# Two load queues at the start, three pairs' normalisation moved to the fourth step, one statistics block moved up in the tail

## What is computed

```
x = x + Wo(softmax(q k^T / 8) v),  q = layernorm(x) Wq,  k = ctx Wk,  v = ctx Wv
logits = layernorm(x) phi_w^T + phi_b            # (8, 56, 64, 32)
D = softmax over slots, C = softmax over experts
Xt = tanh(layernorm(clip(sum over tokens of D * layernorm(x))))
x = x + sum over slots of C * (Xt expert_w + expert_b)
```

## Time and profile before

| | |
|---|---|
| median of 3 runs | 428.83 us (427.79 to 429.29) |
| the profiled execution's own time | 429.79 us |
| its span (first to last instruction) | 428.0 us |
| mean granted clock | 0.996 |
| busy: PE, DVE, ACT, POOL | 98%, 78%, 58%, 39% |

### The profile page before, as it was taken

The page is one execution under the profiler, slowest core; times in us unless marked ns, Lnnn a source line. Parts: engine busy times, 40 slices in busy tenths (PEclk is TensorE's granted clock), DMA queues, the critical chain, the costliest instruction groups (busy, mean ns, idle before and its releaser), DMA issues.

```text
span 428.0 us, 7292 instructions
## 1 busy us (share of the span) xinstructions
PE 417.5 (98%) x2912; PEld 380.0 (89%) x2912; DVE 333.5 (78%) x613; ACT 247.1 (58%) x413; POOL 168.8 (39%) x99
## 2 busy tenths in 40 slices
PE   6999999999999999999999999999999999999987
PEld 4898999999999999889999998889999888999966
DVE  3788847877886768777898779978897899678891
ACT  2577546675566466646664666646755565556652
POOL 4509800516450405031706134536344634436810
PEclk8999999999999999999999999999999999999999
DMA  6401021114021001210110002000110000098000
GB/s 191 141 32 15 20 72 14 36 49 116 14 25 62 20 12 15 73 18 14 14 73 19 14 8 78 21 12 5 11 20 0 14 12 7 26 247 233 2 2 21
DMA packets 15417, 19.03 MB, mean 44 GB/s; under 512 B 4032, under 2 KB 10960, under 8 KB 15384
## 3 DMA queue, kind: packets, MB, share of 16 engines
q1 hardware_dynamic: 15384, 18.57, 17.4%
HBM read 18.31 MB, written 0.26 MB: 43 GB/s over the span
## 4 chain that ended last, share of the span: by engine, by line
PE 73%; DVE 16%; ACT 7%; DMA 1%; POOL 1%; issue 1%; SPq 0%; POOLq 0%; DVEq 0%
PE turned L745 14%; PE acc L765 8%; PE acc L767 7%; PE acc L766 7%; PE scores L729 7%; PE scores L735 7%; PE scores L732 7%; DVE small L1442 5%; DVE pT_l L1452 4%; ACT prob L1192 4%; PE misc L782 3%; PE misc L651 2%; ACT pT_h L1185 1%; PE misc L810 1%; DMA ctx_raw<-in_ctx_dram 1%; PE scores L1105 1%
## 5 line engine op out<-in xcount | busy, mean ns | idle before, releaser
L1185 ACT CAST pT_h<-turned 125x512 fp32r<-125x512 f32 x168 | 95.2, 590 | 123.4 <-PE turned L745 122.7
L1452 DVE TENSOR_TENSOR pT_l<-turned,pT_h 125x512 fp32r<-125x512 f32 x168 | 112.4, 686 | 56.6 <-ACT pT_h L1185 55.6
L1442 DVE TENSOR_REDUCE small<-scores 128x1 f32<-128x500 f32 x168 | 107.7, 673 | 3.7 <-PE scores L735 3.3
L745 PE MATMUL turned<-ident,prob 128*125 128x128 f32 x672 | 94.4, 276 | 2.0 <-DVE pT_l L1452 1.7
L745 PEld LDWEIGHTS turned<-ident,prob 128*125 128x125 f32 x672 | 87.5, 187 | 9.7 <-DVE pT_l L1452 3.9
L765 PE MATMUL acc<-pT_h,ctx_nh 125*128 125x256 f32 (+1 forms) x288 | 94.9, 330 | 0.0
L1192 ACT ACTIVATE prob<-scores,small 128x1500 f32<-128x1500 f32 x56 | 84.9, 1517 | 11.2 <-DVE small L1445 11.0
L767 PE MATMUL acc<-pT_h,ctx_nl 125*128 125x256 f32 (+1 forms) x288 | 86.5, 300 | 0.0
L766 PE MATMUL acc<-pT_l,ctx_nh 125*128 125x256 f32 (+1 forms) x288 | 86.3, 300 | 0.0
L729 PE MATMUL scores<-ctx_th,qk_h 128*128 128x500 f32 x168 | 70.3, 418 | 0.4 <-ACT prob L1192 0.4
L735 PE MATMUL scores<-ctx_th,qk_l 128*128 128x500 f32 x168 | 65.3, 389 | 0.0
(11 more groups left out here) (222 smaller groups left out, 552.6 us busy)
## 6 DMA issues: line engine op xcount, KB each, us to landing
ctx_raw<-in_ctx_dram SPq DMA_DIRECT2D x7, 750.0 KB
rbc<-rden_row SPq DMA_DIRECT2D x15, 128.0 KB, 3.5
rbc<-rden_row SPq DMA_DIRECT2D x8, 192.0 KB, 3.0
eb<-in_L_ffn_expert_b_dram SPq DMA_DIRECT2D x4, 256.0 KB, 5.9
ctx_raw<-in_ctx_dram SPq DMA_DIRECT2D x3, 224.0 KB, 6.0
wq_sb<-in_L_xattn_Wq_dram SPq DMA_DIRECT2D x2, 256.0 KB, 4.8
wk_sb<-in_L_xattn_Wk_dram SPq DMA_DIRECT2D x2, 256.0 KB, 5.9
wv_sb<-in_L_xattn_Wv_dram SPq DMA_DIRECT2D x1, 512.0 KB, 3.5
```

Of the source, the lines that this page charges most:

```text
L745: last = tr(turned[0:CK, m, 128 * c:128 * c + 128], prob[u][:, CK * j:CK * j + CK], ident[:, :])
L1185: nc.scalar.copy(pT_h[0:CK, PLACES[g // NT % 2][t], CPB * k:CPB * k + CPB, :], turned[0:CK, (KB * u + k) % 2, :].rearrange("p (c r) -> p c ...
L1442: m = v.tensor_reduce(bankmax[:, u, k:k + 1], scores[:, k, 0:KW], AX.X, ALU.max)
L1452: v.tensor_tensor(pT_l[0:CK, place, dst, :], turned[0:CK, (KB * u + k) % 2, :].rearrange("p (c r) -> p c r", c=CPB), pT_h[0:CK, place, dst ...
```

## The change

- Loads: SP loads x's first pair alone, Wq's first half, ctx rows 0 to 111 of all chunks in one transfer, the second halves of Wq and Wk, x's other pairs, Wv, Wo. ScalarE's queue issues Wk's first half and ctx rows 112 to 124. A turn of the first ctx waits for both parts of ctx, where it waited for its own chunks and the rest. SP's wait before Wv goes.
- The first weight turned is Wk (ScalarE copies it), then Wq (VectorE). The head pairs come before the first ctx turn; the first x turn goes to bank M0. The fillers are 6 of 128 columns in place of 3 of 256, and one more follows the x turn. VectorE's low query part comes before the second ctx part.
- The other pairs: VectorE's statistics move from the beginning to the step t = 3 of b = 0; POOL adds eps, takes the root and applies them between `split_weights` and `split_ctx(1, 1)`, where it did so before `split_ctx(0, 0)`.
- The tail: `slot_stats(3)` follows `slot_stats(2)`, before the wait for the expert bias and `add_expert_bias(0)`.

```diff
@@ SP
-            sp.dma_start(x_sb[:, :, :], x_v).then_inc(x_in, 16)
+            sp.dma_start(x_sb[:, 0:1, :], x_v[:, 0:1, :]).then_inc(x_in, 16)
             sp.dma_start(wq_sb[:, 0:HW], Wq[:, 0:HW]).then_inc(wq_in[0], 16)
-            sp.dma_start(wk_sb[:, 0:HW], Wk[:, 0:HW]).then_inc(wk_in[0], 16)
-            sp.dma_start(ctx_raw[ROWS0:CK, :, :], ctx_v[0][ROWS0:CK, :, :]).then_inc(ctx0_rest_in, 16)
-            for k in range(KB):
-                chunks = slice(CPB * k, CPB * k + CPB)
-                sp.dma_start(ctx_raw[0:ROWS0, chunks, :], ctx_v[0][0:ROWS0, chunks, :]).then_inc(ctx0_in[k], 16)
+            sp.dma_start(ctx_raw[0:ROWS0, :, :], ctx_v[0][0:ROWS0, :, :]).then_inc(ctx0_in[0], 16)
             sp.dma_start(wq_sb[:, HW:INNER], Wq[:, HW:INNER]).then_inc(wq_in[1], 16)
             sp.dma_start(wk_sb[:, HW:INNER], Wk[:, HW:INNER]).then_inc(wk_in[1], 16)
-            sp.wait_ge(ctx0_in[KB - 1], 16)
+            sp.dma_start(x_sb[:, 1:NQ, :], x_v[:, 1:NQ, :]).then_inc(x_rest_in, 16)
@@ POOL
             root(0, 0, 1)
-            root(1, 1, NQ)
-            pool.wait_ge(ln_rs, 2)
+            split_ctx(0, 0, first=True)
+            split_qk(1)
+            split_weights()
+            pool.wait_ge(rest_mv, 1)
+            gp.tensor_scalar(lnvar[:, 1:NQ], lnmv[:, 1:NQ, 1], EPS, None, ALU.add).then_inc(rest_var, 1)
+            pool.wait_ge(rest_var, 1)
+            gp.tensor_tensor(lnrs[:, 1:NQ], lnvar[:, 1:NQ], neghalf[0:PT, 1:NQ], ALU.pow).then_inc(rest_rs, 1)
+            pool.wait_ge(rest_rs, 1)
             for q in range(1, NQ):
                 last = gp.tensor_scalar(xn[:, q, :], x_sb[:, q, :], lnmv[:, q, 0:1], lnrs[:, q:q + 1],
                                         ALU.subtract, ALU.mult)
             last.then_inc(xn_rest, 1)
-            split_ctx(0, 0, first=True)
-            split_qk(1)
-            split_weights()
             split_ctx(1, 1)
@@ TensorE
-            keep_busy(3)
+            keep_busy(6)
+            pe.wait_ge(wk_in[0], 16)
+            turn_weight(wk_sb, 0, S2)
             pe.wait_ge(wq_in[0], 16)
             turn_weight(wq_sb, 0, S0)
-            pe.wait_ge(wk_in[0], 16)
-            turn_weight(wk_sb, 0, S2)
             pe.wait_ge(xn_ready, 1)
-            turn_xn(0, 1, ACC)
-            turn_ctx(0, 0, 1, first=True)
+            turn_xn(0, 1, M0)
+            keep_busy(1)
             pe.wait_ge(setup_act, 1)
             pe.wait_ge(setup_dve, 1)
             head_pairs(wqT, wkT, 0, T1, S1)
+            turn_ctx(0, 0, 1, first=True)
+            pe.wait_ge(xnT_dve, 1)
             turn_ctx(0, 1, 0, first=True)
             pe.wait_ge(setup_act, 2)
             pe.wait_ge(setup_dve, 2)
-            pe.wait_ge(xnT_dve, 1)
             make_qk(0, ACC)
@@ ScalarE
+            act.dma_start(wk_sb[:, 0:HW], Wk[:, 0:HW]).then_inc(wk_in[0], 16)
+            act.dma_start(ctx_raw[ROWS0:CK, :, :], ctx_v[0][ROWS0:CK, :, :]).then_inc(ctx0_in[1], 16)
...
-            copy_out(1, wqT[:, 0:4, :], S0)
+            copy_out(1, wkT[:, 0:4, :], S2)
+            copy_out(3, wqk[:, 0:8:2, :], T1, SCALE)
             hi_ctx(0, 0, 0, 1)
-            copy_out(3, wqk[:, 0:8:2, :], T1, SCALE)
@@ VectorE
             layernorm(0, x_sb, 0, 1)
-            layernorm(1, x_sb, 1, NQ)
...
                     if first and t == 3:
                         copy_out(14, wvo[:, 9:16:2, :], M1)
+                        dve.wait_ge(x_rest_in, 16)
+                        for q in range(1, NQ):
+                            m = v.bn_stats(lnbuf[:, q, :], x_sb[:, q, :])
+                        m.then_inc(rest_stat, 1)
+                        dve.wait_ge(rest_stat, 1)
+                        for q in range(1, NQ):
+                            m = v.bn_aggr(lnmv[:, q, :], lnbuf[:, q, :])
+                        m.then_inc(rest_mv, 1)
...
-            copy_out(2, wkT[:, 0:4, :], S2)
-            copy_xnT(0, 1, ACC)
+            copy_out(2, wqT[:, 0:4, :], S0)
+            copy_xnT(0, 1, M0)
+            copy_out(4, wqk[:, 1:8:2, :], S1, SCALE)
             lo_ctx(0, 0, 0, 1)
-            copy_out(4, wqk[:, 1:8:2, :], S1, SCALE)
+            lo_qk(0, ACC)
             lo_ctx(0, 0, 1, 0)
-            lo_qk(0, ACC)
             lo_ctx(0, 0, 2, 1)
...
             slot_stats(2)
+            slot_stats(3)
             dve.wait_ge(eb_in, 16 * EPT)
             add_expert_bias(0)
             last_combine_shift_upper()
             add_expert_bias(1)
-            slot_stats(3)
             last_combine_sum()
```

More of the change, by code:

```diff
@@ L217, in xattn_softmoe_kernel @@
         x_in = sem("x_in")
+        x_rest_in = sem("x_rest_in")
         wq_in = [sem(f"wq_in{n}") for n in range(2)]
@@ L222, in xattn_softmoe_kernel @@
         ident_ready = sem("ident_ready")
+        rest_stat = sem("rest_stat")
+        rest_mv = sem("rest_mv")
+        rest_var = sem("rest_var")
+        rest_rs = sem("rest_rs")
         ln_stat = sem("ln_stat")
@@ L233, in xattn_softmoe_kernel @@
         setup_dve = sem("setup_dve")
-        ctx0_in = [sem(f"ctx0_in{k}") for k in range(KB)]
-        ctx0_rest_in = sem("ctx0_rest_in")
+        ctx0_in = [sem(f"ctx0_in{n}") for n in range(2)]
         ctx_in = sem("ctx_in")
@@ L441, in split_ctx @@
                 if first:
-                    pool.wait_ge(ctx0_rest_in, 16)
-                    for k in range(KB):
-                        pool.wait_ge(ctx0_in[k], 16)
+                    for part_in in ctx0_in:
+                        pool.wait_ge(part_in, 16)
                 else:
@@ L600, in _ @@
             split_ctx(3, 1)
-            root(2, 0, 1)
+            root(1, 0, 1)
             split_qk(4)
@@ L607, in _ @@
             combine_shift(0)
-            root(3, 1, 2)
+            root(2, 1, 2)
             split_qk(6)
@@ L616, in _ @@
             combine_shift(1)
-            root(4, 2, 3)
+            root(3, 2, 3)
             split_phi()
@@ L623, in _ @@
             dispatch_scale(2)
-            root(5, 3, 4)
+            root(4, 3, 4)
             pool.wait_ge(x2n_dve, 4)
@@ L645, in turn_ctx @@
                 if first:
-                    pe.wait_ge(ctx0_rest_in, 16)
-                    pe.wait_ge(ctx0_in[k], 16)
+                    for part_in in ctx0_in:
+                        pe.wait_ge(part_in, 16)
                 else:
@@ L689, in keep_busy @@
                 for _ in range(n):
-                    mm(bank(ACC)[:, 0:256].rearrange("p (c r) -> p c r", c=2), ident[:, :],
-                       ident[:, :].unsqueeze(1).broadcast_to([128, 2, 128]), start=True, stop=True)
+                    mm(bank(ACC)[:, 0:128], ident[:, :], ident[:, :], start=True, stop=True)
             def turn_xn(q0, q1, k):
@@ L1486, in residual @@
                 dve.wait_ge(x1_dve, q + 1)
-                layernorm(q + 2, x_sb, q, q + 1)
+                layernorm(q + 1, x_sb, q, q + 1)
             def lo_x2nT(q, k):
@@ L1592, in ffn_step @@
                     q = (b - 3) // 2
[L1593 removed]
+                    layernorm_apply(q + 1, x_sb, x2n, q, q + 1, x2n_dve)
                 if b in (4, 6) and t <= 1:
@@ L1687, in _ @@
             residual(LAST)
-            layernorm_apply(NQ + 1, x_sb, x2n, LAST, NQ, x2n_dve)
+            layernorm_apply(NQ, x_sb, x2n, LAST, NQ, x2n_dve)
             lo_x2nT(LAST, M0)
```

## The result

| | median us | runs | ratio to before | 95% interval |
|---|---|---|---|---|
| before | 428.43 | 4 | | |
| changed | 433.57 | 4 | 1.0098 | 1.0075 to 1.0122 |

A forecast was written before the change was run, and what follows sets the result against it. TensorE's stream was taken to bound the kernel between beginning and tail. Beginning -3.4, POOL's chain +3.7, slack -0.1 gave +0.2; with the tail's -0.8 the sum was -0.6, 428.3 us from 428.83, range 426.6 to 430.6.

The forecast's parts named there:

- the gain of the beginning: Start to VectorE's first row maximum: 11.4 in place of 14.80, 3.4 us earlier, bounds 1.6 to 3.9.
- When the loads land: Beginning: x pair and both weight halves, 568 KB, there at about 4.8; the ctx rows at 6.5 to 7.5.
- ctx complete at 9.8: Beginning, rival: the first turn waits for late ctx, gain only 1.6, time 430.0; chance 0.10.
- The clock: Beginning: head pairs run at the full clock, 1.16 us, from 6.3 to 7.5.
- rival of a second fall at 8.4: Beginning: if turns carry little weight, query product and scores run at low clock, +1.2 us, 429.4; chance 0.08.
- The cost of the moved step: POOL, before the second ctx split: eps addition, root and applies add 3.7 us (3.5 to 4.0).
- This chain already touches the stream: POOL's split, ctx load, broadcast, VectorE, TensorE, to 68.6: slack 0.05 to 0.1, so the beginning's gain is spent, net +0.2.
- The sign by which I wanted to confirm this part: Before normalise(0, 1): VectorE idle about 5 us, TensorE waiting, POOL's split ending at 50.7, broadcast landing at 64.2.
- The clock's fall in the new wait: TensorE at 62 to 68 us, rival: standing still lowers its clock, price 1.7 us, 429.9; chance 0.20.
- The statistics in the fourth step: VectorE, fourth step: pushes row maximum of tile 4 by about 0.5, hidden by the wait; uncovered, 0 to 0.3.
- The tail: End of kernel: fourth statistics block moved earlier, TensorE no longer waits for set 3's tanh; 0.8 us less (0.4 to 1.0).
- the three unfavourable cases: Rivals at beginning and 62 to 68 us: late ctx 0.10, clock falling at 8.4 0.08, clock falling in the wait 0.20.

The follow-up runs named there:

- e7: e4 with all loads of the beginning on SP's one queue, x pair first, then Wk, Wq, the ctx rows: 428.85 us, ratio 0.9987 to before.
- e6: e4 with rows 0 to 111 of the first ctx in three transfers by chunks, each turn waiting for its own: 427.20 us, ratio 0.9969 to before.
- e12: The same kernel as e6, run again: 428.65 us, ratio 0.9980 to before.
- e1: The kernel before with only the tail's slot_stats(3) moved after slot_stats(2): 428.43 us against 429.06, ratio 0.9998.
- e2: The kernel before with only the other pairs' normalisation moved on VectorE and POOL, loads as before: 432.63 us, ratio 1.0095.
- e3: The kernel before with an extra POOL operation of about 1.7 us between the weight split and the second ctx split: 430.22 us, ratio 1.0039.
- e8: e2 (old loads and beginning, moved normalisation) with e4's SP order and e1's tail: 428.33 us, ratio 0.9974 to before.
- e4: The changed kernel, with SP handling group 1's reciprocals of element 0 before the third ctx load: 428.55 us, ratio 0.9992 to before.
- e5: The changed kernel with the other pairs' statistics in step 1 and POOL's work on them before element 1's query split: 429.05 us, ratio 0.9996 to before.
- e11: The changed kernel with 12 filler products where TensorE waits 2.7 us for the second scaling: 432.13 us, ratio 1.0059 to before.
- e9: e6 with more fillers in the beginning (7 for 6, 1 between the weight turns, 2 for 1 before the head pairs): 427.42 us, ratio 0.9952 to before.
- e10: e6 without any filler in the beginning: 430.04 us, ratio 1.0012 to before.

## Why the prediction was wrong

**The step that failed** is the gain of the beginning: "So this stage ends 14.80 - 11.4 = 3.4 us earlier". It measured 0.5, less even than its lower bound of 1.6. The 2.9 us are all lost ahead of the first query product: it starts at 11.33, forecast 8.3, and from there to the row maximum the forecast (3.1) holds (2.9). Two terms were wrong.
- *When the loads land.* Wq's half came at 6.20 (both halves forecast at 4.8), so the head pairs began at 7.73 in place of 6.3. The ctx, for which I took 6.5 to 7.5, was whole at 9.38, near the 9.94 at which POOL could start on it before. The pace was not the error. I took 480 KB by 4.31, which is 177 KB per us; the windows show more, 233 GB/s from 1.6 to 4.3 in the kernel before, and in the changed kernel:

```profile
1.60:6.20 4.60, 3.57 (x17) 3.04 (x17) 0.97 (x4) 1.87 (x2) 0.56 (x1) 1.00 0.90 225
6.20:9.40 3.20, 2.66 (x23) 2.50 (x23) 0.87 (x2) 0.00 (x0) 0.02 (x1) 0.76 1.03 296
```

  The error was to count only the bytes that are needed. By 6.2 some 1.0 MB had moved, where x's pair and the two halves are 568 KB, and by 9.4 some 2.0 MB, where these and the ctx are 1.3 MB: loads issued behind the needed one moved beside it. And for the ctx the forecast did not even use its own pace: 568 + 750 KB at 177 KB per us from 1.6 are there at 9.0, not at 7.5. e7 shows that the second queue adds no pace. The case "ctx complete at 9.8" was the right one for the load, and I had given it 0.10. One part of the change is not tested: SP's wait ahead of Wv is gone, so Wv and Wo (512 KB each) are issued at 3.68 and 4.60 in place of 9.80 and 10.17, beside the ctx. No run has the new order with that wait kept.
- *The clock.* I ran the head pairs at the full clock. In the changed kernel's profile they ran at the low one (window 8 to 12: 0.59), as before: 2.0 us, from 7.73 to 9.7, where I had 1.16, and the eight ctx turns behind them took 1.85 where e6's took 1.07 at the full clock. The rival of a second fall at 8.4 had 0.08. It happened in this run; the e6 and e12 profiles show one kernel without and with it, 1.6 us apart. The condition of that rival, that turns carry little weight, no run isolates: e6 and e12 have the same turns, and the clock fell in one of them. The trace of before was itself an instance of the late beginning: in e1, e2 and e3 the same loads reached the row maximum at 13.40, 13.02 and 13.59, not 14.80. So the 0.5 is itself partly a draw, and the two beginnings can be compared only at like clock. With the head pairs at the low clock the old one reached the row maximum at 14.80 (before) and 14.24 (e8), the new one at 14.15 to 14.36 (changed, e4, e5, e11): nothing to 0.6 us gained. At the full clock the old one has 13.40 and 13.02 (e1, e2), the new one with chunks 12.72 and 12.57 (e6, e9): 0.3 to 0.8; the new one without chunks has no such profile.

**The cost of the moved step was right**, place and size: POOL +3.7 (eps addition 0.24, root 0.89, applies 2.37), the low part of the second ctx, the ctx load, the broadcast, VectorE, TensorE. "This chain already touches the stream" holds: e3's delay of 1.7 us came through as 1.2 (medians) or 1.7 (ratio), and before's VectorE start and the stream were 0.05 apart. What I had as 13.6 us "but a DMA's variation" varies between 12.7 and 13.7. With 3.4 expected in hand the net was +0.2; with 0.5 it is +3.2, which is what step 8 shows. The sign by which I wanted to confirm this part, VectorE idle for about 5 us and TensorE for 2.7, came true (5.39 and 2.74), but it could not have told a gain of 3.4 from one of 0.5: before's idle time of 1.66 plus 3.7 is 5.4, and 3.7 less the slack of 0.98 is 2.7, whatever the beginning does.

**The clock's fall in the new wait** was the slower rival, at 0.20 and 1.7 us. It came: the changed kernel's profile shows it, and so does e2's, behind a wait of 2.29 (TensorE, at 66.31); all four runs of e2 have a mean clock of 0.996 where e3's ten have 1.000. Its price was 0.9 between steps 8 and 9, which is gone in e11's profile, and 0.7 in e2: about half of what I took. Part of the difference is that TensorE would have waited there at the full clock too: in e11 it stands 0.43 at 70.19, for VectorE's low part. What hid the rest no run isolates.

**The statistics in the fourth step** were costed right at nothing: steps 4 and 5 of e2 moved by 0.2 and 0.1, step 6 not. **The tail** was 0.6 to 0.7 for 0.8; bias 2, waiting for the third experts, sets it as described (the product at 417.82 waits 0.23 for it), and the turn of set 3 waits for nobody:

```profile
416.93 0.66 PE L1090 MATMUL scores<-ident,xt 128*128 128x128 f32 x4
417.82 2.53 PE L1107 MATMUL scores<-combT,yt 128*128 128x336 f32 x8 [0.23 <-DVE yt L1720]
```

The sum by what was measured, from step to step: -0.5 + 3.7 + 0.9 - 0.6 = +3.5, the difference of the spans; the ratio of the times, 4.2 (3.2 to 5.2), agrees. Of the 4.1 between this +3.5 and the forecast -0.6, the beginning has 2.9, the clock 0.9, and the rest is small. Besides its size the lesson is in the weights: the three unfavourable cases (late ctx, the clock at the start, the clock in the wait) were priced as alternatives to one another. All three come from loads or a broadcast that are late for TensorE, and they came together.

## What to carry to other kernels

Before a step is moved on an engine that is off the critical path, follow what its new successors release, through the other queues: here a wait in SP's program order put a few KB of reciprocals behind a 750 KB load, and reordering two lines of SP (e4) took away 4.5 us where the compute stayed as late. A gain that rests on loads should be sized from all bytes in flight by then, those issued behind the needed ones too, and it should be checked whether the trace of before is a typical one. Fillers that bridge waits for loads keep the clock (e9 against e10: 2.6 us); in e9 seven of them in front delayed nothing that shows (Wk's turn at 4.78, in e6 with six at 4.75).

## What had not been expected

- A kernel's runs fall in two clusters some 1.5 us apart: 426.8 to 427.6 and 428.3 to 430.3 for one and the same program (e6, e12). In the profiled runs the difference is TensorE's clock in the first 14 us: full from 5 to 6 us on and staying (e1, e2, e6, e9), or falling again near 8 (before, changed, e12), or first recorded as full at 10.4 to 13.8 (e4, e7, e8, e11; e3, at 9.0, stands between). e5 and e10 have no record there. The kernel before has them as well, ten of its 25 runs beside e1 to e4 up to 428.1 and the others from 428.7 on; in its other 56 runs the gap is partly filled (428.1 to 428.7).
- The granted clock reads 1.00 in the windows before its first recorded change, whatever it was: in e4 it reads 1.00 from 5 to 8, but four turns took 1.12 where e6's took 0.66 at the same place. Where no change is recorded at all, as in e10, it reads 1.00 throughout. In that stretch the durations tell, not the column. The window and the timeline of e4:

```profile
5.00:8.00 3.00, 2.65 (x11) 1.95 (x10) 0.99 (x3) 0.59 (x1) 0.18 (x1) 1.00 1.03 265
```
```profile
6.20 1.12 PE L677 MATMUL scores<-ident,wq_sb 128*128 128x128 f32 x4 [0.32 <-DMA wq_sb<-in_L_xattn_Wq_dram]
```

- 56 KB of x alone, issued beside Wk's half, were there no earlier (3.79) than 224 KB had been; with one queue and x in front (e7), at 2.48.
